# Attention blocks on one core: value products in a shared pool of eight banks, with value blocks of 32 columns

## The reference

```python
def attn(x, ctx, wq, wk, wv, wo, bo, heads):
    q, k, v = split(x @ wq), split(ctx @ wk), split(ctx @ wv)   # heads of 8 or 20 columns
    a = softmax(einsum('bhid,bhjd->bhij', q, k) * dh ** -0.5)
    return merge(einsum('bhij,bhjd->bhid', a, v)) @ wo + bo
L0: cross-attention, 20 heads of 8, 512 keys, plus rows
L1: x += self-attention(LN(x)), 256 keys; x += cross-attention(LN(x)); x += gated GELU MLP(LN(x))
L2: two attentions of 8 heads of 20 columns (508 context keys; the last 4 context rows attend to x's rows)
L3: as L1
```

## Time and profile before

| what | value |
|---|---|
| three runs | 920.84, 924.26 (median), 926.18 us |
| the profiled execution | 923.25 us, of which the span from first to last instruction is 921.3 us |
| PE busy | 880.2 us (96%), 7810 products, 7810 weight loads |
| DVE busy | 669.9 us (73%) |
| ACT busy | 654.7 us (71%) |
| value products (L1010) | 2944 records, 199.3 us of PE's busy time; their weight loads 57.4 us |
| copies of finished outputs (L1268) | 116, 45.2 us |

### The profile page before, as it was taken

How to read it: one execution, slowest core, us unless ns; L and a number is a source line. 1 busy time by engine, 2 the same in 40 slices (tenths; PEclk the granted TensorE clock), 3 DMA queues, 4 the chain that set the end, 5 groups by cost and what they waited for, 6 DMA issues and landing times.

```text
span 921.3 us, 21210 instructions
## 1 busy us (share of the span) xinstructions
PE 880.2 (96%) x7810; PEld 594.2 (64%) x7810; DVE 669.9 (73%) x1607; ACT 654.7 (71%) x1423; POOL 55.3 (6%) x92
## 2 busy tenths in 40 slices
PE   8999999999999999999999999999999999999987
PEld 6656565666666577676667776665676666766655
DVE  3978878878788876657566667776777898686822
ACT  7677786877777777667777576676777777776652
POOL 2000000000000000000000000000000000000100
PEclk9999999999999999999999999999999999999999
DMA  8111121111111201001000300001102111111100
GB/s 292 43 36 36 36 47 24 24 29 24 27 44 33 47 22 26 19 18 36 13 1 2 124 3 2 22 11 28 30 19 47 36 32 28 31 36 24 31 9 7
DMA packets 25964, 32.21 MB, mean 35 GB/s; under 512 B 9220, under 2 KB 17416, under 8 KB 25608
## 3 DMA queue, kind: packets, MB, share of 16 engines
q1 hardware_dynamic: 25864, 30.86, 13.1%
HBM read 9.21 MB, written 0.66 MB: 11 GB/s over the span
## 4 chain that ended last, share of the span: by engine, by line
PE 79%; DVE 8%; ACT 8%; issue 4%; ACTq 0%; DVEq 0%
PE pv_ps L1010 17%; PE bank_ps L952 12%; PE bank_ps L972 11%; PE bank_ps L928 8%; PE bank_ps L929 7%; DVE mx L1428 5%; PE bank_ps L1057 5%; PE bank_ps L986 4%; ACT probs L1259 3%; PE bank_ps L1037 3%; PE bank_ps L1130 3%; PE bank_ps L1118 2%; PE bank_ps L1174 2%; ACT oT L1268 1%; PE bank_ps L1076 1%
## 5 line engine op out<-in xcount | busy, mean ns | idle before, releaser
L1428 DVE TENSOR_REDUCE mx<-bank_ps 128x1 f32<-128x512 f32 (+3 forms) x720 | 452.1, 682 | 91.0 <-PE bank_ps L972 89.6
L1259 ACT ACTIVATE probs<-bank_ps 128x512 f32<-128x512 f32 x736 | 380.9, 601 | 116.7 <-PE bank_ps L952 115.2
L1010 PE MATMUL pv_ps<-probs,v 128*9 128x256 f32 (+2 forms) x2944 | 199.3, 376 | 5.4 <-ACT probs L1259 2.3
L952 PE MATMUL bank_ps<-qT,ring 64*128 64x256 f32 x1280 | 171.0, 303 | 2.5 <-DVE gate L1515 1.0
L972 PE MATMUL bank_ps<-ring,qT 64*128 64x512 f32 (+1 forms) x800 | 168.4, 393 | 2.4 <-ACT kdense L1310 1.1
L952 PEld LDWEIGHTS bank_ps<-qT,ring 64*128 64x128 f32 x1280 | 128.6, 185 | 62.7 <-issue 22.3
L972 PEld LDWEIGHTS bank_ps<-ring,qT 64*128 64x128 f32 x800 | 87.3, 184 | 43.2 <-issue 19.6
L1010 PEld LDWEIGHTS pv_ps<-probs,v 128*9 128x9 f32 (+2 forms) x2944 | 57.4, 90 | 76.4 <-issue 22.7
L1310 ACT ACTIVATE kdense<-bank_ps 128x512 fp32r<-128x512 f32 (+2 forms) x116 | 58.3, 556 | 22.2 <-PE bank_ps L1057 21.8
L1234 ACT ACTIVATE ks<-bank_ps 128x320 fp32r<-128x320 f32 x80 | 35.7, 447 | 42.5 <-PE bank_ps L929 22.1
L1452 DVE TENSOR_TENSOR qT<-bank_ps,qT 128x256 fp32r<-128x256 f32 (+1 forms) x108 | 47.0, 436 | 23.6 <-PE bank_ps L986 23.2
(11 more groups left out here) (178 smaller groups left out, 1037.1 us busy)
## 6 DMA issues: line engine op xcount, KB each, us to landing
ring<-kdense SPq DMA_DIRECT2D x240, 64.0 KB, 2.0
ring<-kdense SPq DMA_DIRECT2D x160, 32.0 KB, 1.9
wb<-in_w_blk SPq DMA_DIRECT2D x2, 2240.0 KB, 8.4
wd<-in_w_down SPq DMA_DIRECT2D x2, 400.0 KB, 8.5
x<-in_x SPq DMA_DIRECT2D x4, 160.0 KB, 4.5
bias<-in_bias SPq DMA_DIRECT2D x1, 640.0 KB
out_rows<-x SPq DMA_DIRECT2D x4, 160.0 KB, 1.9
gate<-in_ctx SPq DMA_DIRECT2D x3, 192.0 KB, 4.8
```

Of the source, the lines that this page charges most:

```text
L952: mm = pe.matmul(bank[0:kr, i * a["nq"]:(i + 1) * a["nq"]], key_op(n, h)[:, c * P:c * P + kr], query_rows(u, b, h), start=True, stop=True)
L1010: mm = pe.matmul(pv_ps[32 * j:32 * j + a["dh"] + 1, 0:a["nq"]], v, probs[0:kr, s % N_P, i * a["nq"]:(i + 1) * a["nq"]], start=(c == 0), st ...
L1259: nc.scalar.activation(probs[0:kr, s % N_P, 0:w], bank[0:kr, 0:w], ACT.Exp, scale=float(a["dh"]) ** -0.5).then_inc(free, 1)
L1428: nc.vector.tensor_reduce(mx[b][0:rows, t, heads[0]:heads[-1] + 1:heads[-1] - heads[0] or 1], bank[0:rows, 0:a["hpm"] * a["nk"]].rearrange ...
```

## The change

The fixed bank goes. There are eight banks in the pool, and a quad's first `pv` takes one of them like any other step; it is given back by the copy to `oT`. So `out_full` and `out_taken` go, the planner no longer lets a quad's first value step wait for the copy of the quad before, and it gives the step any of the eight banks. A bank that comes from the pool holds old content, and the copy reads all 128 partitions; so each head's product now writes its 32 partitions in full: the weights are 32 columns that begin at the head's values (its 9 or 21, and what lies behind them), and each chunk of values is 180 columns long with zeros behind the last head. The room for that comes from the first context rows, which are loaded into a slot of `probs` for a start.

```diff
-N_BANK = 7
+N_BANK = 8
+V_CHUNK = 180
...
         if kind == "pv":
             cs = runs(quads[step[1]]["u"])[step[2]]
-            return ([("st", max(s for s in quads[step[1]]["slots"] if slots[s]["c"] == cs[-1]))]
-                    + ([("oev", step[1] - 1)] if step[1] and step[2] == 0 else []))
+            return [("st", max(s for s in quads[step[1]]["slots"] if slots[s]["c"] == cs[-1]))]
...
-                self.banks[bank] = ("low", step) if step[0] in LOW else step
+                self.banks[bank] = ("low", step) if step[0] in LOW else ("oev", step[1]) if step[0] == "pv" else step
...
-    return range(N_BANK) if step[0] in BANKED else ()
+    return range(N_BANK) if step[0] in BANKED or step[0] == "pv" and step[2] == 0 else ()
...
-        v20 = three("v20", [P, 4, 20, 9])
-        v8 = three("v8", [P, 6, 8, 21])
+        v_all = [{8: a, 20: b} for a, b in zip(three("v20", [P, 4 * V_CHUNK + 24]), three("v8", [P, 6 * V_CHUNK]))]
...
-        ctx_n = [ctx_0[:, :, :]] + [gate_cols[:, i * 4 * C:(i + 1) * 4 * C].rearrange("p (t c) -> p t c", t=4) for i in range(B - 1)]
+        ctx_n = [probs[:, N_P - 1, 0:4 * C].rearrange("p (t c) -> p t c", t=4)] + [gate_cols[:, i * 4 * C:(i + 1) * 4 * C].rearrange("p (t c) -> p t c", t=4) for i in range(B - 1)]
...
-                def keep_clock(n):
+                def keep_clock(bank, n):
...
-                        pe.matmul(pv_ps[:, :], ident[:, :], probs[:, N_P - 1, :], start=True, stop=True)
+                        pe.matmul(bank[:, :], ident[:, :], probs[:, N_P - 1, :], start=True, stop=True)
...
-                        if k == 0 and n:
-
-                            pe.wait_ge(S["out_taken"], n)
+                        if k == 0:
+                            out, out_full = take(step)
...
-                                v = values(u, b)[0:kr, c + (4 if u == 4 else 0), h, :]
-                                mm = pe.matmul(pv_ps[32 * j:32 * j + a["dh"] + 1, 0:a["nq"]], v,
+                                at = (c + (4 if u == 4 else 0)) * V_CHUNK + h * (a["dh"] + 1)
+                                mm = pe.matmul(out[32 * j:32 * j + 32, 0:a["nq"]], v_all[instance(u, b) % 3][a["dh"]][0:kr, at:at + 32],
...
-                        act.wait_ge(S["out_full"], n + 1)
+                        bank, free = filled(act, ("pv", n, 0))
...
-                        nc.scalar.activation(dst, pv_ps[:, 0:ATT[u]["nq"]], ACT.Copy).then_inc(S["out_taken"], 1)
+                        nc.scalar.activation(dst, bank[:, 0:ATT[u]["nq"]], ACT.Copy).then_inc(free, 1)
...
-                nc.vector.memset(pv_ps[:, :], 0.0)
+                for v in v_all:
+                    nc.vector.memset(v[8][:, 4 * V_CHUNK:], 0.0)
+                    nc.vector.memset(v[20][:, :].rearrange("p (t c) -> p t c", t=6)[:, :, 8 * 21:], 0.0)
```

More of the change, by code:

```diff
@@ L626 @@
     "negm_ready": {"negm"},
-    "out_full": {"pv_last"}, "out_taken": {"oev"}, "k_high": {"kv_proj", "x_keys", "qkv_proj"}, "x_split": {"x_keys"},
+    "k_high": {"kv_proj", "x_keys", "qkv_proj"}, "x_split": {"x_keys"},
     "q_high": {"q_proj", "ca_q"}, "x_biased": {"x_bias"}, "var_ready": {"ln"},
@@ L650, in build @@
     for step in order:
-        kinds = {step[0]}
-        if step[0] == "pv" and step[2] == len(runs(quads[step[1]]["u"])) - 1:
-            kinds.add("pv_last")
         for name, by in SIGNALS.items():
-            if kinds & by:
+            if step[0] in by:
                 seen[name] = seen.get(name, 0) + 1
                 value[name, step] = seen[name]
-        if step[0] in BANKED:
+        if banks_of(step):
             turn[step] = (place[step], uses[place[step]])
@@ L667, in sem @@
             return ctx.enter_context(nc.semaphore(name))
-        pv_ps = ctx.enter_context(nc.psum_tensor("pv_ps", [P, 512], F32))
         bank_ps = [ctx.enter_context(nc.psum_tensor(f"bank_ps{i}", [P, 512], F32)) for i in range(N_BANK)]
@@ L698, in build @@
         x = [sb(f"x{b}", [P, TQ, D]) for b in range(B)]
-        ctx_0 = sb("ctx_0", [P, 4, C])
         ca_n = two("ca_n", [NCA, C])
@@ L709, in build @@
         kca = two("kca", [P, 2, SQ], FR)
-        v20 = three("v20", [P, 4, 20, 9])
-        v8 = three("v8", [P, 6, 8, 21])
+        v_all = [{8: a, 20: b} for a, b in zip(three("v20", [P, 4 * V_CHUNK + 24]), three("v8", [P, 6 * V_CHUNK]))]
+        v20 = [v[8][:, 0:4 * V_CHUNK].rearrange("p (t c) -> p t c", t=4)[:, :, 0:20 * 9].rearrange("p t (h d) -> p t h d", h=20) for v in v_all]
+        v8 = [v[20][:, :].rearrange("p (t c) -> p t c", t=6)[:, :, 0:8 * 21].rearrange("p t (h d) -> p t h d", h=8) for v in v_all]
         qs20 = two("qs20", [P, TQ, 20, 32], FR)
@@ L788, in build @@
                         if slots[s]["last"]:
-                            used_after[s] = (S["out_full"], step[1] + 1)
+                            at, use = turn["pv", step[1], 0]
+                            used_after[s] = (bank_full[at], use + 1)
                         else:
@@ L1013, in _ @@
                             if slots[s]["last"]:
-                                mm.then_inc(S["out_full"], 1)
+                                mm.then_inc(out_full, 1)
                             else:
@@ L1066, in _ @@
                         if (tag, b) == LAST_FEED:
-                            keep_clock(LAST_WARM)
+                            keep_clock(bank, LAST_WARM)
                         src = natural(tag, b) if tag in LNS else x[b]
@@ L1126, in _ @@
                         last = [q["n"] for q in quads if q["u"] == u and q["b"] == b][-1]
-                        pe.wait_ge(S["out_taken"], last + 1)
+                        taken(pe, ("pv", last, 0))
                         for k, (qd, t, rows) in enumerate(parts_of(u, i)):
@@ L1135, in _ @@
                         if ends(u, b):
-                            keep_clock(1)
+                            keep_clock(bank, 1)
                         for i in range(1 if u == 3 else 3):
@@ L1297, in _ @@
                         split_high(ks8, 0, TQ, P, 20, "k", x[b][:, :, :].rearrange("p t d -> p (t d)"))
-                        nc.scalar.activation(values(4, b)[:, 4:6, :, 0:20].rearrange("p t h d -> p (t h) d"),
-                                             x[b][:, :, :].rearrange("p t (h d) -> p (t h) d", d=20), ACT.Copy).then_inc(S["k_high"], 1)
+                        nc.scalar.activation(values(4, b)[:, 4:6, :, 0:20],
+                                             x[b][:, :, :].rearrange("p t (h d) -> p t h d", d=20), ACT.Copy).then_inc(S["k_high"], 1)
                     elif kind == "k_tr":
```

## The result

The changed kernel takes 964.5 us, the median of four runs (959.36 to 968.08), beside 922.61 us for the kernel before in the same set of runs (920.84 to 926.18). The ratio is 1.0445, with an interval of 1.0385 to 1.0505: 4.5% slower, outside the predicted range and beyond every rival. The profiled execution took 964.39 us, with a span of 962.6.

The account below looks back on a forecast made before the run. TensorE, busy 96% of the span at full clock, was taken to bound the kernel. Terms -5.0 + 3.9 - 4.3 + 3.4 = -2.0 took the profiled 923.25 us to 921.2 us; range 908 to 932.

Parts of the forecast that it names:

- Nothing for the rest: Memsets, the output copy, context rows, clock-keeping products and turning back of outputs: no time gained or lost.
- Passages, -5.0: TensorE's list: changes between kinds of product fall from 746 to 707, saving 5.0 us (3.9 to 7.8).
- 32 columns, +3.9: Value products' weight loads: wider first loads at the openings of 230 runs cost 3.9 us, up to 19.5.
- rival four: Wider weight loads show inside runs of value steps, 13.2 us in place of 3.9: 930.5 us, chance 0.05.
- The wait for the copy, -4.3: Openings of quads' value steps: the 8.6 us wait goes, half returns as exponential waits; saves 4.3 us (0 to 8.6).
- rival one: TensorE's waits go in full, none comes back, passages save at the upper price: 910.8 us, chance 0.27.
- Value steps behind their exponentials, +3.4: Value steps close behind their scores go from 25 to 35; added waits cost 3.4 us (0 to 6.8).
- rival two: ScalarE's queue: exponentials replace copies as the wait, and exponential waits double by 10.0 us: 932.2 us, chance 0.15.
- the doubling that it named as its refutation: Value products' waits for exponentials, 10.0 us before: if they double, the prediction counts itself wrong.
- The pool of eight, 0: Eight pooled banks: no gain, down to -1.2 us; openings waiting for a bank cost nothing, up to +4.3 us.

Follow-up runs that it names:

- ninth experiment: Changed kernel with the planner's copy-wait rule put back and SP's last-context loads and stores issued three key transfers later, against the kernel before: 919.91 us, ratio 0.9941.
- The eighth: Changed kernel with SP's last-context loads and stores three key transfers later and planner constant HANDOFF 250 for 210, against the kernel before: 928.12 us, ratio 1.0006.
- fifth experiment: Changed kernel, same list, with SP alone issuing last-context loads and stores three key transfers later, against the kernel before: 947.43 us, ratio 1.0209.

## Why the prediction was wrong

The forecast was 921.2 us and its highest rival 932.2. The step that failed is the frame of the sum: each wait was priced at its own length, and the clock was taken as it stood in the earlier trace rows; the runs showed a clock that falls to 1.2 GHz behind long waits, 75.1 us in place of 3.5. Under it lies a second omission, in "Nothing for the rest": the list also sets the order in which SP issues key transfers, and the prediction counted the passages and waits of TensorE's order and looked at ACT's and DVE's work, but not at SP's order. Point by point:

- **Passages, -5.0.** Not measured alone. The ninth experiment, with 705 of them, beats the kernel before by 0.6% although it carries the wider loads; but its TensorE also stands 5.1 us less (917.8 - 881.8 = 36.0 us for 41.1), so a gain from the passages is not shown. The eighth, with 769 and few slow stretches, equals the kernel before. Counting them does not tell a list's time.
- **32 columns, +3.9.** It fits: +3.2 us (-0.4 to +6.8), which shuts out the 13.2 us of rival four. A load has a median of 110 ns where 107 was taken, and a step stays 0.43 us: at 790.20 us of the changed kernel sixteen records take 1.07 us, at 792.42 eight take 0.64. The rule of the Trainium skill weighed there, "TensorE: Matmul & The Clock Gate", section "The mechanism", did not decide: loads inside a run stayed hidden although the row group is the same.
- **The wait for the copy, -4.3.** The wait went in full, as rival one had it, but it was never 8.6 us of TensorE standing. The prediction added the row of weight loads (6.4) and that of products (2.2), but each of the products' four stalls stands in both rows (the largest is shown below the list). Where a load waited and no product did, the products ahead were still running. What the wait cost lies between the 2.2 us of the products, whose ends are modelled, and the 6.4 us of the loads.
- **Value steps behind their exponentials, +3.4.** As the prediction counted them, these waits grew by 13.0 us, more than rival two's +10.0, and the doubling that it named as its refutation came. But the same double count is in them: in the changed kernel each of the products' twelve waits for exponentials goes with one of a load. By the products alone the growth is 1.8 us (2.3 to 4.1), by the loads alone 11.2 (7.7 to 18.9); either is the smaller part of 41 us.
- **The pool of eight, 0.** 3.6 us of weight loads waiting for banks, within the bound of +4.3. The turning back of outputs waits 7.6 us in place of 12.6, yet with single waits of up to 2.0 us (2.46 for `oTc`), and behind these the clock falls.
- **SP's order, no term.** Two stalls behind late key transfers, 4.19 and 2.38 us, where the earlier trace rows had no such wait. Moving key transfers ahead took the ratio from 1.0445 to 1.0209 in the fifth experiment, some 22 us (17 by the medians), and gave 21 to 24 us in the ninth; of these some 10 and 6 us, at the price in the next point, go with slow stretches at places where no transfer was moved.
- **The clock, no term.** In runs of one kernel the time at 1.2 GHz can be set against the time lost: the ninth experiment's runs of 918.3 us (mean clock 0.996) and 929.29 us (0.983) differ by 11.0 us, and by 24.3 us at the low level (twice 1 minus the clock, times the time), 0.45 us for each us. The kernel before, 920.62 us at 1.000 and 932.49 at 0.987, gives 0.49, and a line through its runs beside the experiments about 0.47. So 75.1 - 3.5 = 71.6 us more at the low level are worth 32 to 35 us, an estimate a little above TensorE's 30.1 us of longer busy time.

The stall of the kernel before that the earlier trace rows shows as a wait of 1.25 us of the products, in the row of its weight loads:

```profile
891.45 0.98 PEld L1010 LDWEIGHTS pv_ps<-probs,v 128*9 128x9 f32 x24 [1.45 <-ACT oT L1268]
```

In sum: about 30 of the 41 us of span are longer busy time, by the estimate above nearly all of it from the slower clock, and about 11 us are longer standing. Of the slow clock 54.6 us stand behind stalls, some 25 us of time, and 20.5 us, some 10, at a place without one. What the new list gained in passages was not measured apart.

What stays open: what exactly brings the clock down. A stall of 1.69 us in the kernel before, at 638.86, and one of 2.00 us in the fifth experiment passed without a fall, and one of 1.47 us in the changed kernel did not; the falls at 57.6 and 625.7 had no stall ahead. How much of the 11 us each wait is worth was not separated, nor whether a list without any stall would get below 915.86 us.

## What to carry to other kernels

Where a planner's list changes, compare the order on every in-order queue, above all what stands behind a transfer that waits for something else. On an engine that is nearly always busy, look for single long waits, not for the sum of short ones: waits of about 2 us cost nearly twice their length here, because the clock fell behind nearly all of them. If such a wait can't be removed, idle products in it give part of the loss back. Before the waits of two rows are added up, see in the timeline whether they are the same stall.

## What the hardware showed unexpectedly

In the twelve traces, from 20 us on, TensorE had 26 stalls of 1.9 us and more, the longest 4.20, and with 25 of them its clock fell from 2.4 to 1.2 GHz, during the stall or at most 1.7 us after its end. Of 34 stalls of 1.2 to 1.9 us, 11 had a fall within 2.1 us of their end; and 12 of 48 falls had no stall of 1.2 us or more as near ahead. In the changed kernel the low level lasted 3.4 to 17.1 us behind a stall, though TensorE was busy again: at 25.00 for all 17.10 us. The Trainium skill, "TensorE: Matmul & The Clock Gate", section "HAM oscillation — how this bites in real kernels", reckons the penalty at half of the time spent at the low clock; the runs here agree, with 0.45 to 0.49 us lost for each us. Its example is a kernel whose products wait for transfers, as at quads 47 and 113.

A long stall that the profile calls "<-issue" on TensorE can be a transfer that SP issued late: SP's own rows, and the gap ahead of them, told which.
